# One-hot matrix of every second half chunk: built by GpSimd and ScalarE instead of VectorE

## The reference, cut to what matters

```
kj = k[src] + edge_attr @ We          # per edge, 256 wide, 4 heads of 64
vj = v[src] + edge_attr @ We
logits = einsum('ehc,ehc->eh', q[dst], kj) / sqrt(C)
m = segment_max(logits, dst);  ex = exp(logits - m[dst])
agg = segment_sum(vj * ex, dst) / segment_sum(ex, dst)
```

## Time and profile before

| | |
|---|---|
| median of 3 runs | 5051.55 us (5050.83 to 5053.5) |
| the profiled execution | 5044.08 us, its span 5042.3 us |
| mean granted TensorE clock | 0.933 |
| PE busy over the span | 4191.8 us (83%) |
| DVE | 3851.4 us (76%) |
| ACT | 2724.1 us (54%) |
| POOL | 2738.1 us (54%) |
| line 974, the one-hot on DVE | 176 times, 264.0 us, mean 1500 ns |
| line 870, the gathers on POOL | 1760 times, 1821.9 us, mean 1035 ns |

### The profile page before, as it was taken

The page is one execution under the profiler, slowest core; times in us unless marked ns, Lnnn a source line. Parts: engine busy times, 40 slices in busy tenths (PEclk is TensorE's granted clock), DMA queues, the critical chain, the costliest instruction groups (busy, mean ns, idle before and its releaser), DMA issues. The chain is left out here.

```text
span 5042.3 us, 107396 instructions
## 1 busy us (share of the span) xinstructions
PE 4191.8 (83%) x19200; PEld 3376.1 (67%) x19201; DVE 3851.4 (76%) x8465; ACT 2724.1 (54%) x10172; POOL 2738.1 (54%) x2848
## 2 busy tenths in 40 slices
PE   2986999999999999978899999999999943049960
PEld 1555888788778788733688878877877833049960
DVE  3444999999999999955799999999999977202222
ACT  0120677777777777731477777767777741013320
POOL 1011777667667677500677767766767723442235
PEclk9998999999999999999999999999999975579985
DMA  4457877777777777534877777777777723522235
GB/s 85 138 195 225 235 215 215 212 216 215 209 212 216 209 217 216 170 118 143 233 219 215 217 209 215 213 210 212 217 213 214 216 74 104 175 94 70 71 95 152
DMA packets 616287, 920.13 MB, mean 182 GB/s; under 512 B 114501, under 2 KB 477829, under 8 KB 615558
## 3 DMA queue, kind: packets, MB, share of 16 engines
q0 software_dynamic: 154448, 501.87, 34.8%
q1 hardware_dynamic: 378390, 323.25, 22.5%
q10 hardware_dynamic: 82848, 88.64, 4.9%
HBM read 800.89 MB, written 112.53 MB: 181 GB/s over the span
## 5 line engine op out<-in xcount | busy, mean ns | idle before, releaser
L870 POOL DMA_INDIRECT edge_kv<-kvD,edge_ix x1760 | 1821.9, 1035 | 961.9 <-issue 556.5
L909 ACT ACTIVATE edge_w<-edge_vj,edge_ex 128x64 f32<-128x64 f32 x7040 | 1872.0, 340 | 647.3 <-PE edge_pa L950 377.1
L927 PE MATMUL edge_ps<-edge_We,edge_ea 112*128 112x256 f32 x7040 | 1842.4, 384 | 52.3 <-DVE edge_prod L1062 19.0
L927 PEld LDWEIGHTS edge_ps<-edge_We,edge_ea 112*128 112x128 f32 x7040 | 1326.9, 191 | 294.0 <-issue 63.6
L950 PE MATMUL edge_pa<-edge_w,edge_oh 128*128 128x260 f32 x3520 | 1095.5, 393 | 122.2 <-DVE acc L984 94.0
L931 PE MATMUL edge_ps<-acc,edge_oht 128*128 x3520 | 1057.8, 381 | 0.3 <-issue 0.3
L950 PEld LDWEIGHTS edge_pa<-edge_w,edge_oh 128*128 128x128 f32 x3520 | 618.2, 189 | 325.3 <-ACT edge_w L911 165.5
L984 DVE TENSOR_TENSOR acc<-acc,edge_pa 128x260 f32 x1760 | 733.0, 416 | 99.2 <-PE edge_pa L950 46.9
L931 PEld LDWEIGHTS edge_ps<-acc,edge_oht 128*128 128x128 f32 x3520 | 675.0, 192 | 96.5 <-issue 1.7
L1030 DVE TENSOR_TENSOR edge_kj<-edge_kv,edge_ps 128x512 f32<-128x512 f32 x880 | 599.1, 681 | 52.3 <-PE edge_ps L931 23.2
L1062 DVE TENSOR_TENSOR edge_prod<-edge_kj,edge_ps 128x512 f32<-128x512 f32 x880 | 598.9, 681 | 0.0
(11 more groups left out here) (228 smaller groups left out, 3194.7 us busy)
## 6 DMA issues: line engine op xcount, KB each, us to landing
edge_ea<-ea_t_dram SPq DMA_DIRECT2D x1760, 112.0 KB
edge_kb<-relD SPq DMA_DIRECT2D x178, 160.0 KB
edge_kv<-kvD,edge_ix POOLq DMA_INDIRECT x1760
kvD<-nodes_kvs ACTq DMA_DIRECT2D x98, 256.0 KB
exp_xr<-xsD SPq DMA_DIRECT2D x105, 128.0 KB
ysD<-exp_yo ACTq DMA_DIRECT2D x105, 128.0 KB
xsD<-mix_zr POOLq DMA_DIRECT2D x26, 512.0 KB
edge_pen<-penD SPq DMA_DIRECT2D x352, 32.0 KB
```

The costliest lines, as they stand in the source:

```text
L870: nc.gpsimd.indirect_dma_start(out=kv[:, j % HT, :], out_offset=None, in_=g.kvD, in_offset=bass.IndirectOffsetOnAxis(ap=ix[:, h, j % HT:j ...
L909: nc.scalar.activation(w[:, j % 4, h * CA:h * CA + C], vj[:, slot, h * C:(h + 1) * C], ACT.Copy, scale=ex[:, x, h, k:k + 1])
L927: nc.tensor.matmul(ps[:, j % 4, 0:D], ea[:, j % HT, k, :], We[:, k, :], start=(k == 0), stop=(k == 1))
```

## The change

VectorE keeps the one-hot of half 1 (m = 2c - 3, at its pair 0) and no longer makes that of half 0. For half 0 (m = 2c - 2) GpSimd, at its step 14, ahead of the clearing and the gather of that step, subtracts the destination row of each edge from the column number (one tensor_tensor of 128 x 1280 elements, both inputs broadcast in SBUF). ScalarE, at its step 16, ahead of the weighting of that step, turns the difference d into 1 - |d| clipped at zero with two activations over 1280 elements, Abs and Relu, as `keyed` does. Since d is a whole number, the result is the same one-hot. GpSimd's subtraction waits for TensorE's use of the half's former content (`s_ape`, up to its step 5), ScalarE waits for the subtraction (`s_off`), and TensorE's step 16 waits for ScalarE (`s_ohs`); step 6 waits for VectorE as before (`s_oh`, now counted once per chunk).

```diff
+            def offsets(m, par):
+                need(pool, s_ape, HT * m - HT)
+                nc.gpsimd.tensor_tensor(oh[:, par, :, :], g.free[:, :].unsqueeze(1).to_broadcast([P, HT, P]),
+                                        g.relS[:, bass.ds(m * HT, HT)].unsqueeze(2).to_broadcast([P, HT, P]), ALU.subtract).then_inc(s_off, 1)
...
                 for j in range(T):
                     h = j // HT
+                    if j == 14 and lagged(c, 16):
+                        offsets(2 * c - 2, 0)
                     if j % 4 == 2 and (not isinstance(c, int) or 0 <= c * T + j - 14 < NS):
...
+            def onehot(done, par):
+                act.wait_ge(s_off, done)
+                nc.scalar.activation(oh[:, par, :, :], oh[:, par, :, :], ACT.Abs).then_inc(s_abs, 1)
+                act.wait_ge(s_abs, done)
+                nc.scalar.activation(oh[:, par, :, :], oh[:, par, :, :], ACT.Relu, bias=g.ones[:, 0:1], scale=-1.0).then_inc(s_ohs, 1)
...
+                    if j == 16 and lagged(c, 16):
+                        onehot(c, 0)
...
                         if j % HT == 6:
-                            pe.wait_ge(s_oh, 2 * c - (2 if j < HT else 1))
+                            pe.wait_ge(*((s_oh, c - 1) if j < HT else (s_ohs, c)))
...
-                    if j % HT == 0 and lagged(c, j + 6):
-                        onehot(2 * c - (3 if j < HT else 2), 1 if j < HT else 0)
+                    if j == 0 and lagged(c, 6):
+                        onehot(2 * c - 3, 1)
```

More of the change, by code:

```diff
@@ L786, in edges @@
         s_oh, s_w, s_ape, s_acc, s_init = (st.sem(n) for n in ("s_oh", "s_w", "s_ape", "s_acc", "s_init"))
-        s_resc, s_vinit, s_off, s_abs = (st.sem(n) for n in ("s_resc", "s_vinit", "s_off", "s_abs"))
+        s_resc, s_vinit, s_off, s_abs, s_ohs = (st.sem(n) for n in ("s_resc", "s_vinit", "s_off", "s_abs", "s_ohs"))
         s_mt, s_m, s_D, s_et, s_ex, s_Y = (st.sem(n) for n in ("s_mt", "s_m", "s_D", "s_et", "s_ex", "s_Y"))
```

## The result

| | us | ratio to the kernel before (95% interval) |
|---|---|---|
| before | 5050.82 (7 runs, 5047.09 to 5053.5) | |
| after | 5031.17 (7 runs, 5022.77 to 5044.59) | 0.9966 (0.9953 to 0.9979) |
| forecast | 4953, range 4925 to 5015 | |

What follows compares the result with a forecast made beforehand. VectorE's list was taken as the bound, TensorE close behind. 86 chunks x (1.27 - 0.03) = 106.6 us, less 5.5 in the drains is 101, less 3 for late chunks: 5051.55 to about 4953 us, range 4925 to 5015.

Steps and rivals of the forecast that it cites:

- The bound and the one-hot that goes: VectorE's list bounds the edge part; dropping its 1.40 us one-hot, less 0.13 us of wait, gains 1.27 us a chunk.
- undisturbed chunk: Edge-part chunk from one VectorE one-hot to the next chunk's same one: 37.05 us before, 35.78 forecast.
- ScalarE's part: Abs and Relu at step 16, 2.73 us together, end just as wanted: 0.03 us a chunk, 5.5 us in two drains.
- Rival 2: ScalarE's pair is late and TensorE's stall comes back; at 1.2 us of lateness about 5050 us; chance 0.06.
- GpSimd's part: Subtraction at step 14 takes 2.83 us, none on the path; list 34.9 us against 35.78, 0.9 us to spare.
- rival 3: GpSimd reads broadcast operands slowly; from a subtraction of 4.95 us on slower than before, 5144 us at 6 us; chance 0.09.
- 3 us for late chunks: Allowance taken off the whole gain for chunks in which GpSimd comes later than usual: 3 us.
- rival 1: GpSimd becomes the bound; a 3.63 us subtraction blocks VectorE's scan, 0.3 to 0.8 us a chunk: 4980 to 5022 us; chance 0.20.
- the 98 us: Forecast gain of the whole kernel, the median going from 5051.55 to about 4953 us.
- 0.13 us of wait at pair 0: VectorE's kj of pair 0 waits some 0.13 us for two TensorE matmuls, with an estimated 0.05 us semaphore.
- The 0.31 us of reserve: At VectorE's kj of pair 0, the time after its matmuls' start shrinks by 0.31 us, from 0.83 to 0.52.
- the prediction's list: GpSimd's work per chunk (gathers, clearings, index copies, a blocked gather): 32.1 us, 34.9 with the subtraction.

Runs made afterwards that it cites:

- e18_after: The unedited changed kernel once more, on a chip where posts come on time: 4959.02 us, 0.9870 of the kernel before.
- e1_none: Changed kernel with the one-hot of half 0 left out on all engines, TensorE multiplying with zeros, posts on time: 4912.66 us, 0.9771 of the kernel before.
- e9_none: Changed kernel without the one-hot of half 0, on a chip with late posts: 4962.63 us, 0.9830 of the kernel before.
- e3_act: Changed kernel with ScalarE's pair working on zeros and GpSimd's subtraction left out, posts on time: 4926.32 us, 0.9800 of the kernel before.
- e12_act15: Changed kernel with ScalarE's pair at step 15, ahead of the exponential, instead of step 16: 5041.26 us, 0.9993 of the kernel before.
- e11_split2: Changed kernel with GpSimd's subtraction in two pieces, the second at step 2 of the next chunk: 5149.27 us, 1.0198 of the kernel before.
- e2_gps: Changed kernel with GpSimd's subtraction kept and ScalarE's pair left out, posts on time: 4942.32 us, 0.9827 of the kernel before.
- set 1: Four kernels on one chip with posts on time: no one-hot of half 0, each part alone, and one moved wait; the kernel before took 5029.41 us.
- set 5: One chip, posts on time: changed kernel with GpSimd's clearing cut from 1040 to 16 columns (the shorter list), 4928.17 us, beside it unedited, 4959.02 us.
- e14_gps: Changed kernel with the subtraction kept and ScalarE's pair left out, on a chip with late posts: 5170.01 us, 1.0217 of the kernel before.
- e15_act: Changed kernel with ScalarE's pair on zeros and the subtraction left out, on a chip with late posts: 4985.01 us, 0.9847 of the kernel before.
- e10_after: The unedited changed kernel once more, on the same chip as e9_none: 5035.20 us, 0.9970 of the kernel before.
- e16_after: The unedited changed kernel once more, on the same chip as e14_gps and e15_act: 5175.16 us, 1.0235 of the kernel before.
- e13_ix: Changed kernel with GpSimd's index copies two steps ahead of their use, at steps 8 and 18: 5127.29 us, 1.0127 of the kernel before.
- e4_bunch: Kernel e1_none with GpSimd waiting for one more VectorE pair ahead of gather 14: 5022.01 us, 0.9988 of the kernel before.

## Why the prediction was wrong

- **The bound and the one-hot that goes: right.** 35.78 us were forecast for the undisturbed chunk; 35.80 stands in after's profile and 35.79 in e18_after's. The removal alone brought 116.8 and 84.8 us (e1, e9), where 86 x 1.27 = 109 were forecast. Line 989 ran 88 times, as said. What I missed is how few chunks of after are undisturbed: the median of the 79 is 37.14 us, as before.
- **ScalarE's part: right in the chunk and in the drain.** The pair takes 1.26 + 1.36 = 2.62 us (2.73 forecast), and the mean chunk of e3_act is 0.02 to 0.03 us over that of e1_none (2865.0 and 2863.3 us for 79 of them), where I had allowed 0.03. But the spans of the two differ by 4922.1 - 4909.3 = 12.8 us, of which the 79 chunks hold 1.7: some 11 us lie elsewhere. From the last kj addition of a layer to its last addition into the accumulator it is 39.1 and 38.2 us in e1_none, 41.1 in both layers of e3_act: 4.9 us for the two drains, where I had priced 5.5. Another 6.4 us stand between the first kj addition and the first one-hot of the layers (62.0 and 62.3 us against 67.3 and 63.4). I can't put those down to the pair: e9_none, without it, has 68.3 and 67.7 us there. Rival 2 was a late ScalarE; e12_act15 speaks against it, and e11_split2 shows that it would have been dear.
- **GpSimd's part: the step that failed.** Its price was too high rather than too low, 2.336 us against 2.83 (the bounds were 1.30 and 3.63), so rival 3's condition (4.95 us) was far off. What failed is "none of it lies on the path by itself" and that the list fits with 0.9 us to spare. I had asked whether the list is longer than the chunk, and whether the gathered rows come in time. The list stays within the chunk, and waits for gathered rows stay few. But a full list has two prices that I had not on my sum: I had put this term at nothing.
- **First, collisions: mis-sized in kind.** I had placed line 1053 behind the subtraction from one chunk's timeline and took 3 us for late chunks. In the first measurement the scan is 421 ns in the mean against 268 before, 13 us in all; in e2_gps 451 against 255 in e1_none: (451 - 255) x 88 = 17 us, of e2's cost of 29.7. Where GpSimd's list is full, its work drifts against VectorE's, and some chunks meet the scan whatever one timeline says. This was a part of rival 1's mechanism, at about its lower price, though its condition (a subtraction of 3.63 us) was not met: the subtraction costs 29.7 us in set 1, and the shorter list gives 30.9 us back in set 5. The other 12 us of set 1 I can't assign.
- **Second, late posts: not among my rivals.** On the other chips TensorE's posts come late, more of them with the subtraction, and VectorE waits. Between the two profiled executions of the first measurement (5044.08 and 5044.59 us) all of the 98 us is missing; VectorE's waits that end with a post of line 946 rose by 76 us (from 30 to 106), and the scan takes the 13 us named above. On one chip the subtraction costs 185 us (e14_gps over e15_act), of which these waits make 151; on another the two parts together cost 73 (e10_after over e9_none), of which they make 52. Their signs were in the trace of before, where line 931 has 108 late posts, 71 of them by over 1 us, and line 950 has 112, while VectorE has 4 waits for line 931 in layer 1. I took a matmul's end in the timeline for the moment at which VectorE may go on, added 0.05 us for a semaphore, and gave VectorE 0.13 us of wait at pair 0. No row had the 0.05 us; on-time posts stand 0.014 us behind the modelled end in the median, late ones up to 2.6. The 0.31 us of reserve that the change takes away is not the whole of it: e9_none lacks it too and has 32 waits, where e10_after has 92.
- **The chances.** I gave 0.85 to a gain of over 0.2%. Of the five measurements of the changed kernel three show one (0.9966, 0.9970, 0.9870), one shows none (1.0000) and one a loss of 2.35%. The loss that rival 3 gave (5144 us) came at 5175 us by another way.

What stays open. What differs between the chips I can't say: the operations have the same durations on both kinds (the kj addition 681 ns, the gather 946 or 947 ns in the median of e1_none and e9_none). What makes a post late is only narrowed down. In layer 1 of e16_after, of the posts whose matmul ended within the first three gathers since GpSimd's last pause of over 0.45 us, 50 of 512 were late; behind five or more gathers, 216 of 333. Layer 1 of the kernel before shows the same: some 22 of 650 in the first three, some 89 of 273 behind four or more. In e1_none, on a chip with posts on time, none of some 1075 was late in the first three and none of some 500 behind four or more. So late posts go with long unbroken stretches of GpSimd on these chips. That is a correlation, and e13_ix, made to break the stretches by another way, did not break them. Nor does any run tell whether the recording of the profile, which loses records on just these chips, has a part in the lateness. Nor do I know why about as many late posts (779 and 678) end 89 waits of 1.1 us each ahead of the kj addition in e10_after and 142 of 1.6 us each in e16_after, which leaves the changed kernel 73 us above e9_none and 190 us above e15_act. A kernel with pauses kept between the gathers was not tried on a chip with late posts.

## What to carry to other kernels

Moving work to an engine that "has room" may not be free when it fills that engine's list: here GpSimd went from 32.1 to 34.4 us of 35.8 (the prediction's list with the measured 2.336 us), and the gain fell short by a third on the best chip and by more than the whole on the worst. That kept pauses would have saved it is the guess that the runs leave. Compute the reserve of each wait from when the waiter goes on in the trace and not from the producer's modelled end, and look for posts that are late already while nobody waits for them. Time such a change on more than one chip, and look at the rows before you take a time as proof: e4_bunch had the right time for the wrong reason.

## What the hardware did that I had not expected

- The same kernel, unedited, took 4959 to 5175 us on different chips, while the kernel before took 5026 to 5061: with the change the time depends on the chip far more.
- Posts of TensorE up to 2.6 us behind the modelled end of the matmul, two of them 0.12 us apart where the steps are 1.74 us apart; on two of the five chips of the experiments almost none.
- A subtraction of 128 x 1280 on GpSimd with both inputs broadcast in 2.336 us (1.8 ns an element), on all chips within some ns; less than the 2.05 ns that I took from a row. Rival 3's slow broadcast read is not there.
- VectorE's scan of 128 x 128 at 1.77 us in place of 0.47 where a clearing of 1.06 us begins 0.42 us into it and keeps its own time, and an operation on four columns at 0.93 in place of 0.23 us beside a subtraction.
- Semaphore records that go missing on the same chips on which posts are late, in before as in after: some 1840 and 2260 of 3300 are there, on the other chips nearly all.
